# A Mamba-and-attention layer on eight cores: the state sum of the scan stage written as a tree of adds, and the per-head query and key loads released one step earlier

## The reference, cut to what matters

```python
dt = softplus(dt_r @ dt_proj_w.T + dt_proj_b)
dA = exp(dt[..., None] * A)
dBx = dt[..., None] * Bv[:, :, None, :] * xc[..., None]
def step(h, inps):
    dA_t, dBx_t, C_t = inps
    h = dA_t * h + dBx_t
    y = einsum('bdn,bn->bd', h, C_t)      # the sum over 16 states
    return (h, y)
y = ys + xc * D
return y * silu(z) @ out_proj_w.T
```

```python
gv = _gate(x, Wsel_v)
v = einsum('bsd,bhse,hedp->bhsp', x, gv, Wv)
att = softmax(einsum('bhsp,bhtp->bhst', q, k) / sqrt(P), axis=-1)
o = einsum('bhst,bhtp->bhsp', att, v)
```

## Time and profile before

| what | value |
|---|---|
| median of the runs (2 runs, 8271.75 to 8278.46) | 8275.11 us |
| the profiled execution's own time | 8270.92 us |
| its span, first to last instruction, slowest core (core 4) | 8269.3 us |
| spans of the 8 cores | 8209.1 to 8269.3 us |
| DVE busy | 4346.7 us (53%) |
| PE busy | 2895.9 us (35%) |
| ACT busy | 1959.8 us (24%) |

### The profile page before, as it was taken

One profiled execution on the slowest core, in us unless ns is written; L12 is line 12 of the kernel. 1 busy time (PEld: TensorE's weight loads), 2 busy tenths in 40 slices (PEclk: granted clock), 3 DMA queues, 4 the chain that ended last, 5 costly groups with the idle time before them and its releaser, 6 DMA issues.

```text
span 8269.3 us, 41910 instructions; the slowest of 8 cores (8209.1 to 8269.3 us)
## 1 busy us (share of the span) xinstructions
PE 2895.9 (35%) x10957; PEld 1115.5 (13%) x11136; DVE 4346.7 (53%) x3869; ACT 1959.8 (24%) x2902; POOL 339.8 (4%) x639
## 2 busy tenths in 40 slices
PE   6200011000300011000250677777775636647272
PEld 3000000000100000000120222222222212223131
DVE  6399956999299975999430222222222343331414
ACT  4122212222122212222221333333331000021111
POOL 0100010000100010000000000000000000000000
PEclk9655556555755556555675777777777767777686
DMA  2400032000500023000368111111111111111211
GB/s 64 50 0 0 0 43 45 0 0 0 88 0 0 0 24 64 0 0 0 76 81 98 24 21 21 21 21 21 17 20 46 42 45 54 51 52 61 71 54 54
DMA packets 100596, 275.28 MB, mean 33 GB/s; under 512 B 19144, under 2 KB 23500, under 8 KB 99084
## 3 DMA queue, kind: packets, MB, share of 16 engines
q0 software_dynamic: 57168, 178.17, 14.3%
q1 hardware_dynamic: 33980, 77.64, 3.2%
q10 hardware_dynamic: 9216, 16.78, 0.7%
HBM read 321.74 MB, written 63.25 MB: 47 GB/s over the span
## 4 chain that ended last, share of the span: by engine, by line
DVE 40%; PE 28%; DMA 10%; issue 9%; ACT 7%; another core or an unknown queue 2%; SPq 1%; DVEq 1%; ACTq 0%; POOL 0%; POOLq 0%
DVE h_band L715 15%; DVE y_sl L728 11%; PE psF L1275 6%; PE psF L1494 6%; PE psF L1302 5%; ACT attT L1314 4%; DVE h_band L725 3%; PE psF L1693 3%; PE psF L1705 3%; DMA xreD<-xin 2%; PE psF L1289 2%; DMA wzD<-winp_z 2%; DVE xc_a L1546 1%; PE psF L883 1%
## 5 line engine op out<-in xcount | busy, mean ns | idle before, releaser
L715 DVE TENSOR_TENSOR_SCAN h_band<-daD,hcol,dxD 128x512 f16<-128x512 f32 x1024 | 1302.5, 1277 | 2.4
L626 ACT ACTIVATE daD<-dtD,c_A 128x512 f32<-128x512 f32 x1024 | 732.3, 721 | 2209.1 <-DVE h_band L715 2199.0
L593 PE MATMUL psA<-woD,xc_a 128*128 128x512 bf16 x250 | 70.4, 404 | 3171.7 <-DVE xc_a L740 3133.6
L728 DVE TENSOR_REDUCE y_sl<-h_band 128x512 f32<-128x8192 f16 x64 | 885.4, 13834 | 7.0 <-DVE h_band L725 0.5
L1314 ACT ACTIVATE attT<-psF 128x1024 bf16<-128x1024 f32 x512 | 498.6, 1022 | 630.8 <-PE psF L1289 624.9
L1363 DVE TENSOR_TENSOR ost<-psF,rlbG 64x512 bf16<-64x512 f32 x64 | 42.5, 681 | 1130.0 <-DMA rlbG<-lrow 548.2
L1275 PE MATMUL psF<-wvG,act_a 128*128 128x512 bf16 x2000 | 483.5, 393 | 181.8 <-DVE ost L1363 152.1
L1494 PE MATMUL psF<-xc_a 128*128 128x512 bf16 x2002 | 471.4, 397 | 34.6 <-DVE xc_a L1546 31.8
L710 DVE TENSOR_TENSOR dxD<-uD,bb_sb 128x512 bf16<-128x512 bf16 x960 | 408.0, 425 | 95.9 <-DVE h_band L715 3.2
L593 PEld LDWEIGHTS psA<-woD,xc_a 128*128 128x128 bf16 x256 | 22.6, 101 | 3216.5 <-issue 3200.9
L1289 PE MATMUL psF<-qT_aug,kT_aug 65*128 65x512 bf16 x1024 | 384.1, 481 | 206.6 <-ACT attT L1314 203.8
(11 more groups left out here) (214 smaller groups left out, 3423.9 us busy)
## 6 DMA issues: line engine op xcount, KB each, us to landing
xc_a<-wob POOLq DMA_DIRECT2D x128, 256.0 KB, 5.2
wzD<-winp_z POOLq DMA_DIRECT2D x64, 256.0 KB, 3.9
woD<-woutT POOLq DMA_DIRECT2D x64, 256.0 KB, 4.9
wob<-wo POOLq DMA_DIRECT2D x1, 16384.0 KB, 301.4
wvG<-wv POOLq DMA_DIRECT2D x32, 512.0 KB, 6.8
xc_a<-w1b POOLq DMA_DIRECT2D x64, 256.0 KB, 7.7
xc_a<-w2b ACTq DMA_DIRECT2D x64, 256.0 KB, 8.9
xreD<-xin SPq DMA_DIRECT2D x16, 512.0 KB, 6.0
```

The costliest lines, as they stand in the source:

```text
L626: inc(s.activation(daD[n % 2][:], dt[:], AF.Exp, scale=c_A[:, dc * NN + n: dc * NN + n + 1]), "da")
L715: last = v.tensor_tensor_scan(h_band[:, n * TW:(n + 1) * TW], daD[n % 2][:], dxD[n % 2][:], hcol[:, dc * NN + n: dc * NN + n + 1], op0=OP. ...
L728: fy = inc(v.tensor_reduce(y_sl[:], bass.AP(h_band[:].tensor, h_band[:].offset, [h_band[:].ap[0], [1, TW], [TW, NN]]), axis=AX.X, op=OP.ad ...
```

## The change

Two edits. In the scan stage, the multiplication of the whole band and the strided sum are replaced. There are now 16 multiplications of one slot each (512 columns), and 15 additions of one slot each that fold the 16 slots in a tree: 16 to 8, 8 to 4, and 4 to 2, of which one goes to `y_sl` in f32, and a last addition into `y_sl`. The tree works in place in `h_band`, so the partial sums are held in 16-bit float. In the attention stage, SP waits for one count less of "gt" before it loads the next head's queries and keys.

```diff
-                fg = inc(v.tensor_tensor(h_band[:], h_band[:], cb_sb[:],
-                                         op=OP.mult), "vf")
-                wge(v, "vf", fg)
-                fy = inc(v.tensor_reduce(
-                    y_sl[:],
-                    bass.AP(h_band[:].tensor, h_band[:].offset,
-                            [h_band[:].ap[0], [1, TW], [TW, NN]]),
-                    axis=AX.X, op=OP.add), "vf")
+                fg = [0] * NN
+                for n in range(NN):
+                    fg[n] = inc(v.tensor_tensor(h_band[:, n * TW:(n + 1) * TW],
+                                                h_band[:, n * TW:(n + 1) * TW],
+                                                cb_sb[:, n * TW:(n + 1) * TW],
+                                                op=OP.mult), "vf")
+                fl1 = [0] * 8
+                for i8 in range(8):
+                    wge(v, "vf", fg[2 * i8 + 1])
+                    if i8 >= 1:
+                        wge(v, "vf", fl1[i8 // 2])
+                    fl1[i8] = inc(v.tensor_tensor(
+                        h_band[:, i8 * TW:(i8 + 1) * TW],
+                        h_band[:, 2 * i8 * TW:(2 * i8 + 1) * TW],
+                        h_band[:, (2 * i8 + 1) * TW:(2 * i8 + 2) * TW], op=OP.add), "vf")
+                fl2 = [0] * 4
+                for i4 in range(4):
+                    wge(v, "vf", fl1[2 * i4 + 1])
+                    if i4 >= 1:
+                        wge(v, "vf", fl2[i4 // 2])
+                    fl2[i4] = inc(v.tensor_tensor(
...
+                wge(v, "vf", fl2[1])
+                f30 = inc(v.tensor_tensor(h_band[:, 0:TW], h_band[:, 0:TW],
+                                          h_band[:, TW:2 * TW], op=OP.add), "vf")
+                wge(v, "vf", fl2[3])
+                f31 = inc(v.tensor_tensor(y_sl[:], h_band[:, 2 * TW:3 * TW],
+                                          h_band[:, 3 * TW:4 * TW], op=OP.add), "vf")
+                wge(v, "vf", f31)
+                fy = inc(v.tensor_tensor(y_sl[:], y_sl[:], h_band[:, 0:TW],
+                                         op=OP.add), "vf")
...
             if h >= 1:
-                wge(sync, "gt", GT_H * h)
+                wge(sync, "gt", GT_H * h - 1)
```

More of the change, by code:

```diff
@@ new lines, in _ @@
+                for i4 in range(4):
[3 more added lines that the diff above has]
+                    fl2[i4] = inc(v.tensor_tensor(
+                        h_band[:, i4 * TW:(i4 + 1) * TW],
+                        h_band[:, 2 * i4 * TW:(2 * i4 + 1) * TW],
+                        h_band[:, (2 * i4 + 1) * TW:(2 * i4 + 2) * TW], op=OP.add), "vf")
+                wge(v, "vf", fl2[1])
+                f30 = inc(v.tensor_tensor(h_band[:, 0:TW], h_band[:, 0:TW],
+                                          h_band[:, TW:2 * TW], op=OP.add), "vf")
```

## The result

The changed kernel takes 7867.17 us (median of 11 runs, 7838.71 to 7915.4) beside 8280.44 us for the kernel before (10 runs). The ratio is 0.9489, 95% interval 0.9464 to 0.9515: 5.1% faster, against the forecast's 5.2%. The profiled execution took 7857.12 us, with a span of 7855.2 us on core 6; before it was 8270.92 us. The forecast of 7841 us and its range of 7805 to 7950 us hold. Executions in which the cores of one die clearly ran longer at a lower granted clock are left out of the medians and ratios.

A forecast was written before the change was run, and what follows sets the result against it. DVE was taken to bound the kernel, with 40% of the chain that ended last. 399 us (scan stage) plus 33 us (head borders) off 8270.9 us gave 7839 us, forecast as 7841 us; range 7805 to 7950 us.

The forecast's parts named there:

- the large term: Scan stage: 16 multiplications and 15 additions take 12.22 us instead of 18.46 us per block, saving 399 us over 64 blocks.
- The small term: Attention stage, head borders: SP's earlier loads shorten PE's wait, saving 33 us over 15 borders; bounds nothing to 40 us.
- The path in the scan stage: Scan stage: other engines stand behind DVE, so what DVE saves in a block shortens the span one for one.
- The price of a start: DVE, 512-column 16-bit operations: 0.34 us per start if nothing needed is late, 0.53 us if waiting for the instruction just ahead.
- The f32 output at 16-bit inputs: Scan stage, addition into y_sl: taken as 0.69 us plus 0.11 us for its waiting successor, 0.80 us; lower bound 0.53 us.
- No new late engine: Scan stage: ACT keeps some 16 us idle at a block's end, PE and POOL have no work inside blocks; nothing comes late.
- PE's gap falls from 9.86 to 7.94 us: Head border: with earlier loads DVE's second scaling starts 1.92 us earlier, shortening PE's gap before the next V projection.
- With the mean gap of 10.14 us: 15 x (10.14 - 7.94) = 33 us: Attention stage: the shorter gap, counted from the mean wait at 15 head borders, saves 33 us in all.
- the border gives nothing: Rival, head border: POOL's DMA takes 5.3 us or more anyway, hiding SP's earlier start; 7872 us, chance 9%.

The follow-up runs named there:

- the run with the added waits: The changed kernel with each of the 16 multiplications made to wait for the one ahead: 8064.94 us, ratio 0.9729 to the kernel before.
- the wide tree: The changed kernel with one multiplication of 8192 columns and four wide additions (4096, 2048, 1024, 512 columns): 7708.55 us, ratio 0.9302 to the kernel before.
- the loads alone: The kernel before with only SP's wait one count earlier: 8293.14 us beside 8300.68 us, ratio 0.9992.
- the early tile: The kernel with four wide additions, PE's first V tile of each head waiting only for DVE's scaling of chunk 2, not 3: 7728.25 us, ratio 0.9299.

## Why the prediction was right, point by point

The mechanism of the large term is right, and it carries the total. The small term is wrong in mechanism, and the range was wide enough to hold it.

- *The path in the scan stage.* Right: DVE's saving came out of the span one for one. 6.37 us x 64 = 408 us per block arithmetic, 404 us on core 4 (the last matmul of L593 starts at 3630.2 us instead of 4033.9).
- *The price of a start.* Right, 0.34 and 0.53 us, shown over a run of 16 and by the run with the added waits. The tree's term came out 9 us larger than written (408 against 399).
- *The f32 output at 16-bit inputs.* Right: L753 took 0.69 us, the upper of the two bounds.
- *No new late engine.* Right, down to the wide tree.
- *The border: the step "PE's gap falls from 9.86 to 7.94 us".* Right, 7.99. *The step "With the mean gap of 10.14 us: 15 x (10.14 - 7.94) = 33 us"* failed. It took a shorter wait for a shorter head. The mean gap did fall to 8.02 us and the waits by 32 us, but the stage became only 8 us shorter on core 4, and the loads alone gave a ratio of 0.9992. What came in its place is 0.7 us more in the V projection and 0.7 us more in the rest of each head, at the lower clock level. The prediction did not ask what clock PE would have behind a shorter gap. The bounds of this term (nothing to 40 us) hold it. The rival "the border gives nothing" named 7872 us, nearer to the median of 7867 us than the forecast, but its mechanism (a slow spreading DMA) was wrong: the DMA took 4.00 us.
- *What is left.* The two profiled slowest cores are not the same. On core 4, from the last product to the end of the span, it took 2002 us before and 1974 us after; on core 6 it was 1964 and 1992 us. The change touches nothing there. Such differences of 28 us between executions are of the size of the border's term, and hide it in the total. That the total came within 26 us of the forecast is therefore a test of the tree's 400 us, and of the border's 33 us it says nothing.

## What to carry to other kernels

A sum across slots that lie far apart is worth replacing by additions of contiguous halves, as wide as they can be: 13.9 us became 5.3 us per block. (What the 16-bit partial sums do to the accuracy was not measured here.) Every cut of an instruction costs: 0.06 to 0.07 us each for independent pieces (0.84 and 1.04 us for 15 cuts), and 0.19 us more where a piece waits for its neighbour. Where PE idles for some microseconds between matmul groups, a shorter wait may buy much less than its length (8 to 16 of 33 us here). Look at the granted clock behind the gap, and try to keep PE busy to its end: here that gave 50 us of the stage, and filler that ended 4.25 us early gave nothing. Judge such a change by periods and stages on one undisturbed core, since the total of eight cores scatters by more.

## What the runs showed of the hardware that I had not expected

- The granted clock rose to 1.00 about 1 us before the product ended and stood there for 2.3 to 2.5 us of PE's idle time. It came back 12.5 to 12.7 us behind the product, whether the V projection had begun 8.0 or 10.1 us behind it (but for three borders of the kernel before), and also where 60 transposes (3.51 us, some 58 ns each) had run in between.
- Transposes whose results nobody reads keep the clock at 1.00 as long as they fill the gap: 125 of them took 7.14 us at 1.00, and the V projection behind them began at 1.00.
- Heads of different inner timing take the same 105.8 us: gaps of 7.7, 8.0 and some 9.9 us go with V projections of 31.9, 31.6 and 30.6 us. In each the clock comes back equally long after the product; why it does so was not settled.
- In many executions some cores show periods some 3 us or more longer in a few of their heads: 106 to 109 us beside 102.4 us with the early tile, but also 108.5 to 109.5 us beside 105.8 us in the wide tree (cores 6 and 7). So they come without added work of PE too. In the profiled execution with 125 transposes no core shows any behind its first head.
